# Another order for the opening of a recurrent tower: on GpSimd the deviation comes first and the bias two items late; on the other engines the first six steps get orders of their own

## The reference

```python
x = embedding[tokens] + pos_enc[:S][None]
for l in range(L):                      # L = 4; S = 256, D = 192
    h = layernorm(x) * g + b
    u, v = split(h @ Wi.T + bi)
    uc = causal depthwise convolution of u, 4 taps, + cb
    delta = softplus(uc @ wd.T + bd);  Bm = uc @ wB.T + bB;  Cm = uc @ wC.T + bC
    state[t] = state[t-1] * exp(-delta[t]) + uc[t] * Bm[t]
    y[t] = sum(state[t] * Cm[t]) * sigmoid(v[t])
    x = x + (y @ wo.T + bo)
h = x + attention(layernorm(x));  out = h + int8_ffn(layernorm(h))
```

## Time and profile before

| | |
|---|---|
| median of 3 runs | 1570.99 us (1569.74 to 1573.64) |
| the profiled execution's own time | 1572.42 us |
| its span, first to last instruction | 1570.2 us |
| TensorE busy | 1494.2 us, 95% of the span |
| VectorE / ScalarE / GpSimd busy | 1347.7 / 1242.8 / 850.5 us |
| mean granted TensorE clock | 0.979 |

### The profile page before, as it was taken

One profiled execution on the slowest core, in us unless ns is written; L12 is line 12 of the kernel. 1 busy time (PEld: TensorE's weight loads), 2 busy tenths in 40 slices (PEclk: granted clock), 3 DMA queues, 4 the chain that ended last, 5 costly groups with the idle time before them and its releaser, 6 DMA issues.

```text
span 1570.2 us, 36660 instructions
## 1 busy us (share of the span) xinstructions
PE 1494.2 (95%) x11441; PEld 1212.6 (77%) x11441; DVE 1347.7 (86%) x3200; ACT 1242.8 (79%) x2686; POOL 850.5 (54%) x1400
## 2 busy tenths in 40 slices
PE   4799999999999999999999997999999999999996
PEld 3678878888888888888888886677777777777763
DVE  5899999999999999999999986688888878888764
ACT  4678879898888888888888864778878777877863
POOL 7888855453335443333333245666666666666642
PEclk9899999999999999999999997999999999999998
DMA  5634201000000000000000000000000000000000
GB/s 113 141 61 83 31 1 34 1 35 0 0 1 1 1 1 0 0 1 1 1 0 0 1 1 2 2 8 12 12 16 11 11 11 11 11 11 16 11 12 26
DMA packets 24445, 27.16 MB, mean 17 GB/s; under 512 B 3104, under 2 KB 22432, under 8 KB 24352
## 3 DMA queue, kind: packets, MB, share of 16 engines
q1 hardware_dynamic: 16672, 19.70, 4.0%
q0 software_dynamic: 7680, 6.30, 3.2%
HBM read 14.58 MB, written 6.29 MB: 13 GB/s over the span
## 4 chain that ended last, share of the span: by engine, by line
PE 69%; POOL 11%; ACT 8%; DVE 6%; issue 6%; DMA 0%; ACTq 0%; DVEq 0%; POOLq 0%
PE banks L723 9%; PE banks L741 7%; PE banks L986 7%; PE banks L732 6%; PE banks L954 6%; POOL x L455 5%; PE banks L911 5%; PE banks L938 5%; PE banks L925 4%; PE banks L846 3%; PE banks L814 2%; PE banks L897 2%; PE banks L1010 2%; PE banks L850 2%; PE banks L900 2%
## 5 line engine op out<-in xcount | busy, mean ns | idle before, releaser
L1691 DVE TENSOR_REDUCE mx<-banks 128x4 f32<-128x1024 f32 x192 | 234.1, 1219 | 45.5 <-PE banks L925 45.1
L1297 ACT ACTIVATE probs<-banks 128x1024 f32<-128x1024 f32 x192 | 195.8, 1020 | 85.4 <-PE banks L938 81.9
L521 POOL TENSOR_TENSOR x<-x,bo_row 128x768 f32<-128x768 f32 (+1 forms) x64 | 120.1, 1876 | 129.0 <-DVE ucr_r L1552 129.0
L723 PE MATMUL banks<-ht,w_uv 128*128 128x512 f32 x576 | 171.2, 407 | 14.2 <-ACT sv_l L1271 12.2
L497 POOL TENSOR_TENSOR lnt<-mv,const 128x4 f32<-128x4 f32 x64 | 27.2, 425 | 267.3 <-DVE mv L1517 267.3
L1543 DVE SCALAR_TENSOR_TENSOR uc_h<-u_h,vec,uc_h 128x512 f32<-128x512 f32 x192 | 154.1, 803 | 2.2 <-ACT uc_h L1204 2.2
L723 PEld LDWEIGHTS banks<-ht,w_uv 128*128 128x128 f32 x576 | 107.2, 194 | 47.8 <-issue 20.9
L723 PE MATMUL banks<-ht,w_uv_rest 128*128 128x512 f32 x384 | 121.4, 398 | 0.0
L938 PE MATMUL banks<-q_t,k_t 64*128 64x256 f32 x768 | 109.3, 336 | 7.4 <-ACT probs L1297 5.9
L1543 DVE SCALAR_TENSOR_TENSOR uc_l<-u_l,vec,uc_l 128x256 f32<-128x256 f32 x192 | 104.1, 542 | 7.8 <-issue 2.9
L1526 DVE SCALAR_TENSOR_TENSOR xs<-x,rstd,xs 128x192 fp32r<-128x192 f32 x256 | 93.6, 425 | 18.3 <-ACT xs L1248 18.3
(11 more groups left out here) (189 smaller groups left out, 4719.3 us busy)
## 6 DMA issues: line engine op xcount, KB each, us to landing
out_dram<-y_out SPq DMA_DIRECT2D x32, 192.0 KB, 2.0
x<-pos SPq DMA_DIRECT2D x12, 384.0 KB, 4.2
raw_z<-w_z_dram SPq DMA_DIRECT2D x4, 704.0 KB, 5.5
raw_uv<-w_uv_dram SPq DMA_DIRECT2D x4, 576.0 KB, 4.0
q_t<-mx_t SPq DMA_DIRECT2D x64, 6.0 KB
emb<-w_qkv_dram SPq DMA_DIRECT2D x1, 864.0 KB, 7.5
w_o<-w_o_dram SPq DMA_DIRECT2D x1, 768.0 KB, 5.2
x<-embedding_dram,idx POOLq DMA_INDIRECT x48, 4.3
```

What stands on the lines that cost most here:

```text
L521: nc.gpsimd.tensor_tensor(rows, rows, bo_row[:, l, :][:, None, :].broadcast_to([P, CT, D]), ALU.add).then_inc(x_biased, 1)
L723: last = nc.tensor.matmul(out[:], w, r[:], start=(k == 0), stop=(k == len(passes) - 1))
L1297: act.activation(probs[:, (s + g // 2) % 2, g % 2, :].rearrange("p (j k) -> p j k", j=2), B_SST, ACT.Exp, scale=float(DH) ** -0.5).then_in ...
L1691: nc.vector.tensor_reduce(mx[:, s].rearrange("p t (j h) -> p j t h", j=2)[:, :, :, g], B_SS.rearrange("p j (t k) -> p j t k", t=2), AX, AL ...
```

## The change

Four things change, all in layer 0 or at its end.

1. GpSimd's order is one for all of layer 0: deviation of item k+1, fetch of item k+3, bias of item k-2. Steps 14 and 15 make up for the lag (items 12 and 13, then 14 and 15). From step 6 to step 14 the bias of item k-2 also waits until that item's `uc` is ready.
2. `OPENING` is 5, so that the orders of the opening hold for steps 0 to 5 in place of 0 to 4.
3. ScalarE takes in the opening `decay` ahead of `save_turned`, as in later steps; `gates` and `round_uc` stay ahead of `round_rows`, now in steps 4 and 5 too.
4. VectorE's opening has one order: taps, `save_y` and `residual`, `rest_of_uc`, `rest_of_rows`, `recurrence` of item k-3, and `measure` of item k+1 last. In step 6 the recurrence is left out, since item 2's was done in step 5.

Layer 0 is written out for 8 steps in place of 6.

```diff
@@ -282,8 +282,8 @@
         def steps(eng, step, fetches=False):
 
 
-            LEAD = 6
             for l in range(L):
+                LEAD = 8 if l == 0 else 6
 
                 for k in range(NCH if fetches and l == 0 else LEAD):
                     m = l * NCH + k
@@ -314,7 +314,7 @@
             return min(n + k, ITEMS) if isinstance(n, int) else n + k
 
 
-        OPENING = 4
+        OPENING = 5
 
 
         PREP_SUMS, PREP_MEANS, PREP_CENTRE, PREP_ROUND, PREP_SPLIT = 2, 3, 4, 5, 5
@@ -508,7 +508,7 @@
                 wait(pool, ln_step, LN * n + 6)
                 nc.gpsimd.tensor_tensor(rstd[:, s, :], y, a, ALU.mult).then_inc(rstd_ready, 1)
 
-            def bias_rows(it):
+            def bias_rows(it, prompt):
                 if it is None:
                     return
                 n, l, c, s = it
@@ -516,7 +516,7 @@
                     pool.wait_ge(s_bo[l], 16 * (L - 1 if l else 1))
                 wait(pool, xs_ready, n + 1)
 
-                wait(pool, uc_ready, n if isinstance(n, int) and n < OPENING else n - 1)
+                wait(pool, uc_ready, n - 1 if prompt else n + 1)
                 rows = x[:, bass.ds(c * CT * D, CT * D)].rearrange("p (k d) -> p k d", d=D)
                 nc.gpsimd.tensor_tensor(rows, rows, bo_row[:, l, :][:, None, :].broadcast_to([P, CT, D]),
                                         ALU.add).then_inc(x_biased, 1)
@@ -602,18 +602,20 @@
             fetch(2)
 
             def step(at, l, k):
-                if l == 0 and k < OPENING:
-
-                    inverse_deviation(at(-1))
-                    fetch(k + 3)
-                    bias_rows(at(0))
-                    return
-
-
-                if l == 0 and FIRST <= k + 3 < NCH:
-                    fetch(k + 3)
+
                 inverse_deviation(at(-1))
-                bias_rows(at(0))
+                if l == 0:
+
+                    if k + 3 < NCH:
+                        fetch(k + 3)
+                    if k < NCH - 1:
+                        bias_rows(at(2), k <= OPENING)
+                    if k >= NCH - 2:
+                        bias_rows(at(1), True)
+                    if k == NCH - 1:
+                        bias_rows(at(0), True)
+                else:
+                    bias_rows(at(0), True)
                 if (to := prepared(l, k, PREP_SUMS)) is not None:
                     weight_sums(to)
                 if (to := prepared(l, k, PREP_SPLIT)) is not None:
@@ -1340,18 +1342,16 @@
                 first_tap(at(2), 1)
                 save_u(at(2), 0)
                 first_tap(at(2), 0)
-                if l == 0 and k is not None and k < OPENING:
-
-                    save_turned(at(1))
-                    decay(at(3))
+                decay(at(3))
+                save_turned(at(1))
+                if l == 0 and k is not None and k <= OPENING:
+
                     save_c(at(3))
                     gates(at(2))
                     round_uc(at(2))
                     if k > 0:
                         round_rows(at(0))
                 else:
-                    decay(at(3))
-                    save_turned(at(1))
                     round_rows(at(0))
                     save_c(at(3))
                     round_uc(at(2))
@@ -1780,27 +1780,19 @@
                         nc.vector.memset(gain_rows[:], 1.0 / D).then_inc(mean_spread, 1)
                         measure(2)
                     other_taps(at(2), (0, 1, 2))
+                    save_y(at(4))
+                    residual(at(4))
                     rest_of_uc(at(2), 1)
                     rest_of_uc(at(2), 0)
-                    if k == 1:
+                    if k > 0:
                         rest_of_rows(at(0))
-                    elif k == 2:
-                        measure(3)
-                        rest_of_rows(at(0))
-                    elif k == 3:
-                        recurrence_products(item(0))
-                        rest_of_rows(at(0))
-                        recurrence_scan(item(0))
-                        recurrence_rest(item(0))
-                        measure(4)
-                    elif k == 4:
-                        save_y(at(4))
-                        residual(at(4))
-                        rest_of_rows(at(0))
-                        measure(5)
+                    recurrence(at(3))
+                    if k > 1:
+                        measure(k + 1)
                     return
                 rows_there(at(-1))
-                recurrence(at(4))
+                if l > 0 or k != OPENING + 1:
+                    recurrence(at(4))
                 statistics(at(-1))
                 statistics_there(at(-1))
                 if early and k == 0:
```

## The result

The changed kernel takes 1585.94 us, the median of 6 runs (1584.52 to 1587.98). Against the kernel before on the same chip the ratio is 1.0075, with an interval of 1.0057 to 1.0093: slower by some 12 us, and outside the range of 1563.5 to 1574.5. The ratio is that of the fast executions; one of the kernel before took 1990.01 us. The profiled execution took 1584.52 us, its span is 1582.7, 12.5 longer than before.

The account below looks back on a forecast made before the run. GpSimd and TensorE were taken to bound layer 0 together, GpSimd limiting the gain. Sums' end -2.2, clock +2.85, saved -2.4 gave -1.75 us: 1569.2 us against the median 1570.99, range 1563.5 to 1574.5 for 8 in 10.

Parts of the forecast that it names:

- The stop in step 5: TensorE's 6.10 us stop in the opening goes; some 2.5 us in step 6 instead, item 6's transposes near 103.5.
- the ring: Opening's closed chain from an item's rows through gates, rounding, recurrence and first tap to the next rows: 14.3 us a turn.
- The biases of the opening now fall beside scans, so I charge nothing for them: Opening: GpSimd's biases beside VectorE's scans cost 0, read from a scan of 0.66 us beside a subtraction.
- From step 6 on the variances are early: Layer 0 from step 6: GpSimd's deviations no longer wait for VectorE's variances, so no wait is added.
- held-up scans: Rival, chance 0.06: biases of items 1 and 2 hold up scans; sums 1.8 us later, 0.0 in all, 1571.
- +1.5 waits: GpSimd in the opening: deviations wait for variances, 0.5 us for item 5 and 1.0 for item 6.
- the 201.5 of the forecast: End of GpSimd's weight sums: 203.7 - 3.7 for two biases less + 1.5 of waits.
- with the same neighbours as after the change: Argument against the faster rival: GpSimd's 13.31 us step, six steps into the steady part, already has these neighbours.
- blocked by its own new order: Rival, chance 0.13: deviations waiting for variances keep fetches back; a turn of 17 us gives sums at 209.1, 1577.
- transfers land late: Rival, chance 0.06: VectorE waits for rows from item 8 on; up to 2 us more, +0.2 in all, 1571.2.
- The end of layer 0: TensorE's restart at the product of the sums: +2.85 us for half clock, -2.4 saved as VectorE and ScalarE caught up.
- Both must come earlier: Weight sums: GpSimd and TensorE arrive together, so layer 1 moves forward only if both do; TensorE 11 us, GpSimd 2.2.

Follow-up runs that it names:

- e_after_tiny: The changed kernel with layer 0's bias added to only 8 of 192 columns of each tile and nothing in its place: 1568.08 us, ratio 0.9942 to before.
- bias-second kernel: The changed kernel with layer 0's bias right behind the deviation in steps 6 to 12, still two items behind: 1577.74 us, ratio 1.0026 to before.
- the pair with GpSimd relieved: Changed kernel and kernel before, each with layer 0's bias on 8 of 192 columns only, nothing in its place: 1568.08 us (0.9942) and 1564.02 us (0.9925).
- e_after_tiny_sums_first: The changed kernel with layer 0's bias on 8 of 192 columns and step 12's weight sums ahead of item 15's fetch: 1564.75 us, ratio 0.9942.
- e_write_only: The changed kernel with layer 0's bias on 8 of 192 columns and a 1400-column memset of an unused tile behind it: 1567.82 us, ratio 0.9954.
- e_pool_old: The changed kernel with GpSimd's order, bias and wait as in the kernel before, the other engines' new orders kept: 1576.12 us, ratio 1.0000.

## Why the prediction was wrong

**The stop in step 5** is gone, as said, and one in step 6 takes its place: 4.08 us in place of some 2.5, with a granted clock of 0.50 behind it (100.9 to 104.7), so that item 6's transposes come at 108.9, not 103.5. The deviation of item 6 was done at 95.3 and not at 92.2, since the biases had held up the work ahead of its variance; without them, in `e_after_tiny`, these transposes come at 104.4. From item 3 to 5 the ring turned in 14.6 and 15.8 us, not 14.3. Ahead of item 5 all is about right: 88.4 against 100.9 before.

**The step that failed** is "The biases of the opening now fall beside scans, so I charge nothing for them", and with it "From step 6 on the variances are early". I had read one row, a scan of 0.66 us beside a subtraction, as proof that scans are never held up. A scan at its usual length beside a GpSimd instruction proves little, for the scan may have come first. Here the scans had begun ahead of the subtraction, at 237.62, and the subtraction took 2.65 for its two halves, against 2.38 in the bias-second kernel above. That fits a GpSimd that had to wait for the scan, but it isn't shown. The Trainium skill, page "SBUF — State Buffer", section "Who interferes with whom", had it right: two SBUF inputs on VectorE contend with a GpSimd instruction that reads SBUF, whatever the operation, and not with one that only writes. The runs here agree on both: one scan of 3.31 in place of 0.66 and a pair of 3.59 in place of 1.26 beside biases, and taps of 0.45 and 0.74 inside a memset.

**The size of that step.** I had given held-up scans as a rival worth 1.8 us, since I looked for biases only in the opening. But the bias costs in every step of the layer: 2.6, 2.9 and 2.9 us at the ends of steps 6 to 8, and from step 9 on 2.2 us on the tap ahead of the variance, so that the variance is late too. The term was "+1.5 waits" for GpSimd; it measured 10.7: 3.08, 1.84 and 1.83 in the opening, three times 1.33 later. The sums end 8.9 us behind the 201.5 of the forecast for it. Besides, what VectorE lost made its steps and TensorE's 15.0 to 15.7 us, so TensorE came late too: it waited 0.92 us at the product, not 9. I had seen that the length of GpSimd's step would be multiplied, but I had it run "with the same neighbours as after the change", and the neighbours are what the change altered; and I had not asked what VectorE, busy 49.42 us of 50, could spare.

**The rival "blocked by its own new order"** named the right queue, a deviation that waits for a variance with the fetch behind it, and sums at 209.1; they ended at 210.4. Its cause was to be a turn of 17 us in the opening. The turn was shorter than that, and most of the wait came from the hold-ups.

**The rival "transfers land late"** is in the trace once: VectorE waits 2.95 us for the rows of item 8, at 106.24, and no more after that. In the pair with GpSimd relieved the same wait (2.93) is one of three in which the lead goes.

**The end of layer 0.** I took 2.4 us as saved and 2.85 as the clock's cost. In fact the way from item 12 to 16 is 68.2 us in place of 60.2, so that nearly half of the miss lies here: item 16's transposes come 14.0 us later than before (269.87 against 255.88), 6.7 of it at the end of the sums and 7.3 behind that, where I had 0.45. Two things that I had put at nothing stand in it: the sums as the last of a step that now begins with the deviation, so that they come a fetch later and starve a tap, and two biases ahead of the weight split in step 15. The runs show both in the trace (14.8 against 20.8, and 14.6 against 17.2); what each is worth in the total is below what these runs tell apart.

**"Both must come earlier"** was true and is not the whole of it. Even with GpSimd relieved the opening's lead of 9.9 us at item 5 is 2.6 us at item 12. In that pair the opening's lead is already 2.7 us at item 7, a step that the prediction took for a steady one: item 7's transposes follow item 6's by 16.8 us, not 13.5.

**Open.** Why the sums' better place doesn't show in the median of `e_after_tiny_sums_first`. Whether a hold-up of the same length costs less at a place where no variance stands behind it: the versions with short steps also have shorter hold-ups. A version in which VectorE reads one operand from elsewhere wasn't tried.

## What to carry to other kernels

When GpSimd's work moves, list what VectorE does beside it at the new place: an instruction that reads two SBUF tiles can be held for the whole of a GpSimd instruction that reads SBUF (2.0 to 2.9 us here beside a bias), while the statistics (1.13 us) and a product that reads PSUM (0.74) take no longer beside a bias than elsewhere. Ask what VectorE can spare: here nothing, so every turn became longer by what was held, and GpSimd, whose next input came from VectorE, had to wait as well. A lead won at the start of a pipeline is worth only what is left of it at the first stage that bounds it; follow one event per item through both kernels before adding it to the total. Rotating a loop's order leaves the middle as it is and moves the ends.

## What the runs showed of the hardware

Several GpSimd instructions in a row can starve one VectorE instruction for all their length: 7.75, 6.39 and (in `e_write_only`) 4.49 us beside the weight sums and what stands ahead of them. In the kernel before the same sums, begun while taps were already running, alternate with them, 1.0 to 1.5 us each; what decides between the two is not shown:

```profile
196.93 1.31 DVE L1543 SCALAR_TENSOR_TENSOR uc_h<-u_h,vec,uc_h 128x512 f32<-128x512 f32 x1
197.66 1.27 POOL L479 TENSOR_TENSOR sums_low<-raw_uv,gain 64x384 f32<-64x384 f32 x1
199.13 1.31 DVE L1543 SCALAR_TENSOR_TENSOR uc_h<-u_h,vec,uc_h 128x512 f32<-128x512 f32 x1
```

What is held also lasts longer than the bias by itself: 1.84 us alone, 2.40 behind a transfer, whose record it overlaps, and 2.0 to 2.9 us lost on VectorE. And GpSimd's step of the same twelve instructions took 13.3 to 13.5 us in the kernel before and 13.8 to 13.9 in `e_pool_old`, with no wait in either: its length isn't set by its own instructions alone.
